# Eight heads scored and mixed in a row over one ring of seven PSUM banks, and a weight fetch placed anew, in a six-layer decoder

## The reference

```python
def attn_layer(x, Wqkv, qs, ksc, Wo):          # HEADS 16, DIM_HEAD 64, WINDOW 64
    q, k, v = split_heads(x @ Wqkv)
    q, k = l2norm(q) * qs, l2norm(k) * ksc
    q, k = rotary(q), rotary(k)                # tables of cos and sin, with a scale along the tokens
    out = local_attention(q, k, v)             # each token sees the 64 before it
    return out @ Wo

def ffn_layer(x, g, bln, W1, b1, W2, b2):      # DIM_INNER 682
    xn = layernorm(x) * g + bln
    a, gate = split(xn @ W1 + b1)
    return a * gelu(gate) @ W2 + b2

for i in range(6):
    x = attn_layer(shift_tokens(x), Wqkv[i], q_scale[i], k_scale[i], Wo[i]) + x
    x = ffn_layer(shift_tokens(x), ln_g[i], ln_b[i], W1[i], b1[i], W2[i], b2[i]) + x
return x
```

## Time and profile before

| | us |
|---|---|
| median of 3 runs | 2654.38 (2652.9 to 2655.96) |
| the profiled execution, its own time | 2655.91 |
| its span, first to last instruction | 2654.1 |
| TensorE busy | 2580.1 (97%), 25160 matmuls |
| VectorE busy | 2279.5 (86%) |
| ScalarE busy | 2059.5 (78%) |
| GpSimd busy | 1388.8 (52%) |
| mean granted TensorE clock | 0.994 of full speed |

### The profile page before, as it was taken

One profiled execution on the slowest core, in us unless ns is written; L12 is line 12 of the kernel. 1 busy time (PEld: TensorE's weight loads), 2 busy tenths in 40 slices (PEclk: granted clock), 3 DMA queues, 4 the chain that ended last, 5 costly groups with the idle time before them and its releaser, 6 DMA issues.

```text
span 2654.1 us, 77750 instructions
## 1 busy us (share of the span) xinstructions
PE 2580.1 (97%) x25160; PEld 2294.4 (86%) x25160; DVE 2279.5 (86%) x7689; ACT 2059.5 (78%) x6056; POOL 1388.8 (52%) x1438
## 2 busy tenths in 40 slices
PE   8889999999999999999999999999999999999996
PEld 7768888888888888888888888888888888888885
DVE  5579989988998888899888989988999998888883
ACT  5458878877887788788778878877887887787774
POOL 5454546455554645455454545545454555556560
PEclk9989999999999999999999999999999999999998
DMA  5212232424222333322234232243323242311100
GB/s 167 80 53 94 72 98 92 159 75 151 92 71 98 125 127 107 118 89 75 94 135 158 71 118 89 75 148 125 113 71 116 84 150 64 102 32 31 42 25 28
DMA packets 149542, 253.25 MB, mean 95 GB/s; under 512 B 21418, under 2 KB 88202, under 8 KB 148106
## 3 DMA queue, kind: packets, MB, share of 16 engines
q1 hardware_dynamic: 148698, 250.90, 29.1%
q10 hardware_dynamic: 688, 0.39, 0.0%
HBM read 137.14 MB, written 80.55 MB: 82 GB/s over the span
## 4 chain that ended last, share of the span: by engine, by line
PE 88%; DVE 3%; issue 2%; DMA 1%; POOL 1%; ACT 1%; SPq 1%; DVEq 0%; ACTq 0%; POOLq 0%
PE ring L1133 29%; PE ring L1183 14%; PE acc L1158 10%; PE score L1224 7%; PE ring L1237 6%; PE acc L1196 6%; PE ring L1147 6%; PE mix L1251 4%; PE mix L1255 2%; PE mix L1253 2%; PE ring L1167 1%; DMA xn<-res 1%; PE ring L1115 1%; PE acc L1203 0%; DVE probs L1609 0%
## 5 line engine op out<-in xcount | busy, mean ns | idle before, releaser
L1133 PE MATMUL ring<-w_qkv,xT 128*128 128x512 f32 x3456 | 883.0, 400 | 5.4 <-DVE with_sin L1516 4.0
L1133 PEld LDWEIGHTS ring<-w_qkv,xT 128*128 128x128 f32 x3456 | 624.0, 189 | 131.8 <-DVE with_sin L1516 5.4
L1418 POOL TENSOR_SCALAR sums_sq<-sums_sq 128x8 f32<-128x8 f32 x384 | 108.5, 283 | 1052.2 <-DVE sums_sq L1511 1043.9
L1354 ACT ACTIVATE probs<-probs,shift 128x128 f32<-128x128 f32 x1536 | 596.6, 392 | 26.5 <-DVE shift L1593 25.8
L1593 DVE CUSTOM_DVE_ANT_0 probs<-score,mask,query_scale 128x128 f32<-128x128 f32 x1536 | 438.7, 347 | 42.4 <-PE score L1224 35.0
L1183 PEld LDWEIGHTS ring<-nT,w_up 128*128 128x128 f32 x3168 | 395.8, 189 | 21.5 <-issue 6.8
L1183 PE MATMUL ring<-nT,w_up 128*128 128x256 f32 x3168 | 409.6, 282 | 4.3 <-issue 3.6
L1299 ACT ACTIVATE with_sin<-ring 128x512 f32<-128x512 f32 x384 | 228.2, 595 | 213.4 <-PE ring L1133 213.4
L1427 POOL TENSOR_TENSOR sums_sq<-sums_sq,half 128x8 f32<-128x8 f32 x192 | 324.4, 1690 | 16.0
L1424 POOL TENSOR_TENSOR query_scale<-sums_sq,half 128x8 f32<-128x8 f32 x192 | 318.0, 1656 | 22.0 <-POOL sums_sq L1418 11.8
L1372 ACT COPY probsT<-ring 128x512 f32<-128x512 f32 x384 | 226.1, 594 | 108.4 <-issue 103.0
(11 more groups left out here) (153 smaller groups left out, 4419.8 us busy)
## 6 DMA issues: line engine op xcount, KB each, us to landing
w_parts_scratch<-staging SPq DMA_DIRECT2D x120, 519.0 KB, 3.1
staging<-in_w_next SPq DMA_DIRECT2D x60, 519.0 KB, 4.9
w_qkv<-w_parts_scratch SPq DMA_DIRECT2D x20, 1536.0 KB, 9.4
v_mid<-v SPq DMA_DIRECT2D x192, 128.0 KB, 2.3
w_up<-w_parts_scratch SPq DMA_DIRECT2D x20, 640.0 KB, 6.9
y_in<-y_scratch SPq DMA_DIRECT2D x48, 256.0 KB, 3.0
res<-y_scratch SPq DMA_DIRECT2D x48, 256.0 KB, 2.8
y_scratch<-res SPq DMA_DIRECT2D x41, 256.0 KB, 3.2
```

Of the source, the lines that this page charges most:

```text
L1133: last = pe.matmul(bank(item)[:], xT[a][:, h, t * P:(t + 1) * P], w_qkv[w][:, h, c, g, :], start=(h == 0 and (a, w) == PASSES[0]), stop=(h ...
L1354: last = act.activation(probs[:, k, cols], probs[:, k, cols], ACT.Exp, bias=shift[:, k, i:i + 1], scale=-1.0, accum_out=sums[:, k, i:i + 1])
```

## The change

Three PSUM tensors go (two `score`, one `mix`) and their banks join the ring, which has seven now. The scores of a quad take two places in it, a mix takes one. `probs`, `probsT`, `shift` and `sums` hold eight heads instead of four. In `PE_ORDER` two quads are scored in a row, and behind them two are mixed in a row: at the start of a slot quads 0 and 1 are scored and quads 2 and 3 of the slot before are mixed; in the middle quads 2 and 3 are scored and quads 0 and 1 mixed. The lists of all engines are ordered anew around this. The first chunk of a slot's pair is loaded at the end of the slot before. The rotary tables are double, loaded at the start of the switch slot, and multiplied on GpSimd. The added tokens of the last layer (`x2`) are loaded ahead of `rest_parts`. `fetch(0)` moves behind the three shifted copies. The item `gelu_table` in `ACT_ORDER` has no instruction of its own.

```diff
-RING = 4
+RING = 7
 PE_ORDER = [
-    ("scores", 0), ("mix", 3), ("unit", 1, 0), ("unit", 1, 1), ("project_out", 0), ("unit", 1, 2), ("unit", 1, 3),
...
+    ("scores", 0),
+    ("scores", 1), ("mix", 2), ("mix", 3), ("unit", 1, 0), ("unit", 1, 1), ("unit", 1, 2), ("unit", 1, 3), ("project_out", 0),
+    ("project_out", 1), ("unit", 1, 4), ("unit", 1, 5), ("input",), ("turn", 1, 2), ("turn", 1, 0), ("turn", 1, 1),
+    ("turned", 0, 0), ("turned", 0, 1), ("turned", 1, 0), ("unit", 0, 0), ("turned", 1, 1), ("turn", 1, 3), ("norm_turn",),
+    ("scores", 2),
+    ("scores", 3), ("mix", 0), ("mix", 1), ("unit", 0, 1), ("gate", 0), ("gate", 1), ("unit", 0, 2), ("gate", 2), ("value", 0),
...
+RING_BANK = [_at % RING for _at in range(len(RING_FILLS))]
...
-    def load_chunk(self, sp, layer, chunk, h):
-        wait(sp, self.chunk_stored, self.chunk_at(layer, chunk, 0) * 32 + 1)
-        sp.dma_start(self.chunk_views(h)[0], self.D["w_next"][layer][:, chunk + h, :]).then_inc(self.raw_loaded, 16)
+    def load_chunk(self, sp, layer, chunk, h, first=False):
+        if not first:
+            wait(sp, self.chunk_stored, (self.chunk_at(layer, chunk, h) - 1) * 32 + 1)
+        sp.dma_start(self.chunk_views(h)[0], self.D["w_next"][layer][:, chunk + h, :]).then_inc(self.raw_loaded[h], 16)
...
+def build_tables(eng, layer, scales_loaded, tables_loaded, tables_built, tables, qk_scales):
+    eng.wait_ge(scales_loaded, layer * 16 + 16)
+    eng.wait_ge(tables_loaded, layer * 16 + 16)
+    for part in range(2):
+        scale = qk_scales[:, part].unsqueeze(1).broadcast_to([P, TILES, 2, HEAD_DIM // 2])
+        for k, sc in ((0, scale), (1, scale[:, :, ::-1, :])):
+            made = tables[layer % 2][:, 2 * part + k].rearrange("p t (a b) -> p t a b", a=2)
+            last = eng.tensor_tensor(made, made, sc, ALU.mult)
+    last.then_inc(tables_built, 1)
...
-        score = [ctx.enter_context(nc.psum_tensor(f"score{i}", [P, GROUP], FP32)) for i in range(2)]
-        mix = ctx.enter_context(nc.psum_tensor("mix", [P, 2, TOKENS], FP32))
...
+                if s.switch == "projections":
+                    load_tables(s.layer + 1)
+                    load_scales(s.layer + 1)
                 if s.early and not (isinstance(n, int) and n == -1):
...
-                    for h in range(SLOT_CHUNKS):
-                        W.load_chunk(sp, s.layer, s.chunk, h)
-                if s.switch == "projections":
-                    fetch(0, s.layer)
-                    load_scales(s.layer + 1)
+                    if isinstance(n, int) and n == 1:
+                        W.load_chunk(sp, s.layer, s.chunk, 0, first=True)
+                        W.load_chunk(sp, s.layer, s.chunk, 1, first=True)
+                    else:
+                        W.load_chunk(sp, s.layer, s.chunk, 1)
                 if s.ffn:
                     wait(sp, acc_read, f * 2 + 1 + 1)
...
                     sp.dma_start(xn[0:1, 1, P:DIM], res[P - 1:P, 0, P:DIM]).then_inc(shifted, 16)
+                if s.switch == "projections":
+                    fetch(0, s.layer)
...
+                if s.chunk is not None and s.more:
+                    W.load_chunk(sp, s.layer, s.chunk + SLOT_CHUNKS, 0)
...
+                elif kind == "scores":
+                    pe.wait_ge(scores_masked, n * HEADS + QUAD_HEADS * item[1] + QUAD_HEADS)
+                elif kind == "mix":
+                    k = item[1] if item[1] < 2 else item[1] - 4
+                    pe.wait_ge(out_split, n * PAIRS + 2 * k + 2)
...
-                wait(pe, scores_masked, H)
-                pe.sem_inc(passed, 1)
+                for half in range(2):
+                    bank_free(s, item, half)
+                    pe.sem_inc(passed, 1)
...
+                if s.switch == "projections":
+                    build_tables(pool, s.layer + 1, scales_loaded, tables_loaded, tables_built, tables, qk_scales)
                 for item in POOL_ORDER:
```

More of the change, by code:

```diff
@@ L79 @@
+    ("turned", 3, 1),
 ]
 ACT_ORDER = [
[L81 to L84 removed]
@@ L88 @@
+    ("copied", 2, 1), ("scale", 3, 0), ("value", 2), ("unit", 0, 5), ("turn", 0, 2), ("turn", 0, 1), ("turn", 0, 0),
     ("turn", 0, 3), ("copied", 3, 0), ("copied", 3, 1),
@@ L138, in is_filled @@
         return -1 <= n < STEPS - 1
-    if kind == "turned":
+    if kind in ("turned", "scores") or kind == "mix" and item[1] < 2:
         return 0 <= n < STEPS
@@ L217, in run_slots @@
             slot(Slot(layer * BATCH + 1, layer, next_batch=2, ffn_batch=0, chunk=0 if layer < DEPTH - 1 else None, new=True))
-        with eng.Fori(1 if layer and not apart else 2, BATCH - 1) as b:
+        with eng.Fori(1 if layer and not apart else 2, BATCH - 2 if apart else BATCH - 1) as b:
             slot(Slot(layer * BATCH + b, layer, next_batch=b + 1, ffn_batch=b - 1, chunk=(b - 1) * SLOT_CHUNKS if layer < DEPTH - 1 else None))
+        if apart:
+            b = BATCH - 2
+            slot(Slot(layer * BATCH + b, layer, next_batch=b + 1, ffn_batch=b - 1, chunk=(b - 1) * SLOT_CHUNKS if layer < DEPTH - 1 else None,
+                      more=False))
         if layer < DEPTH - 1:
@@ L850, in layers @@
         qk_scales = sb("qk_scales", [P, 2, 2, HEAD_DIM // 2])
-        tables = sb("tables", [P, 4, TILES, HEAD_DIM])
+        tables = [sb(f"tables{i}", [P, 4, TILES, HEAD_DIM]) for i in range(2)]
         y_in = T["y_in"]
@@ L1223, in quad_scores @@
                             at = k * BAND + (w // 2) * P
-                            last = pe.matmul(score[side][sides[w % 2], at:at + P], qT[rows, pair, w * WINDOW:(w + 1) * WINDOW],
+                            last = pe.matmul(bank(item, side)[sides[w % 2], at:at + P], qT[rows, pair, w * WINDOW:(w + 1) * WINDOW],
                                              kT[rows, pair, first:first + P], start=True, stop=True)
@@ L1378, in copy_out @@
                     wait(act, attn_projected, s.n)
[L1379 removed]
+                act.copy(oT[0][:, pair:pair + 2, :], wide_bank(("mix", item[1]))).then_inc(out_high, 2)
             def slot(s):
```

200 lines of the change are left out of this document (91 added, 109 removed).

## The result

The changed kernel takes **2719.64 us** (median of 4 runs, 2719.17 to 2720.84), the kernel before 2654.64 (4 runs, 2652.9 to 2655.96): ratio 1.0244, 95% interval 1.0231 to 1.0256. It is slower, as forecast, but by 65 us and not by 20; 2719.6 lies outside 2650 to 2700. The profiled execution took 2720.84, its span is 2718.9.

What follows compares the result with a forecast made beforehand. TensorE's list of work was taken to bound the slot (busy 51.22 of 51.57 us). Terms of -26 - 4 - 2 + 52 = +20 gave 2674 us, 0.7% slower, range 2650 to 2700.

Steps and rivals of the forecast that it cites:

- Part 4: Five layer-switching slots: TensorE waits 8.5 us for the later weight fetch, low clock costs 1.9; 10.4 a slot, +52 us.
- part 3: New waits on ScalarE: 0.34 before the second head pair, 0.86 before the quad 2 scores; +1.20 us a slot.
- part 5: Small terms: five switch slots' excess gone, -4 us; other excess, -2; bank for quad 3 scores has 0.6 us in hand.
- The -2: Earlier chunk load, earlier last-layer output addition and split semaphores remove part of the other 3.8 us excess: 0 to -4.
- Part 1: Every slot: fewer passages through scores and mixing, two joined passages saving 0.51 each; -1.02 us a slot.
- Part 2: Every slot: old waits at the mixing, the scaled heads and the normalized rows go; -0.75 us a slot.
- Net of parts 1 to 3: -0.57: Change per slot without the fetch: a slot of 51.0 us, -26 us over 46 slots.
- C: Rival: VectorE becomes the bound, slots stay at 51.6 or above, the fetch comes on top; up to 2705, chance 0.10.
- A: Rival: the fetch in the switch slots is not waited for; 2622 us, chance 0.13.
- B: Rival: ScalarE is not late and the fetch costs its lower bound; slots of 50.2, 2626 us, chance 0.07.
- D: Rival: both sides cancel, -0.9 a slot and 8 us fetch wait without clock loss; within 6 us of before, chance 0.08.

Runs made afterwards that it cites:

- Experiment 1: The run fetch_first: the changed kernel with only fetch(0) back at its old place, 2673.59 us.
- split_late_root: knot_root with VectorE's first split of the weights moved behind the rotation of unit (0, 1): 2644.29 us, ratio 0.9964 to the kernel before.
- fetch_first: The changed kernel with fetch(0) back ahead of the wait for the attention addition, nothing else: 2673.59 us, ratio 1.0066 to the kernel before.
- knot_three: Kernel of experiment 3 with the scale_ahead edit, two ScalarE copies made sooner, and VectorE's first weight split behind the normalization's application: 2660.72 us.
- split_late: knot_three with VectorE's first split of the weights moved behind the rotation of unit (0, 1): 2650.72 us, ratio 0.9991 to the kernel before.
- gpsimd_lighter: fetch_first with two of GpSimd's query-scale roots replaced by a cheap operation, so the reference is not computed: 2668.76 us.
- knot_root: knot_three with one query-scale root on GpSimd moved behind the root of the normalization: 2650.99 us, ratio 0.9983 to the kernel before.
- experiment 3: fetch_first with the scores' wait for the copied turns placed behind the two waits for free banks: 2657.22 us, ratio 1.001 to the kernel before.
- scale_ahead: Kernel of experiment 3 with ScalarE scaling head pair (0, 1) behind unit (1, 3) and no longer behind the input: 2653.36 us.
- experiments 7 to 10: The four runs knot_three, knot_root, split_late and split_late_root, reordering VectorE's and GpSimd's lists: 2660.72, 2650.99, 2650.72 and 2644.29 us.

## Why the prediction was wrong, point by point

**Direction and the largest term: right.** Part 4 gave 10.4 us a switch slot and +52. Measured: slots of 62.46, 62.69, 62.24, 62.30 and 62.31, 10.1 to 10.5 above the 52.17 of ordinary ones, +49.9 against the same intervals before. By its pieces, 8.5 of idle time and 1.9 of clock were forecast, and 9.10, 9.6, 9.1, 8.8, 8.8 of idle time came out. In the first of them TensorE is busy 52.70, 2.03 more than in the ordinary slot; the unit, the transposes and the turn behind it account for it (2.73 + 0.84 + 0.86 between starts, against 1.48 + 0.44 + 0.44). So the low clock costs about 2.0, and 0.8 of that is not seen in the length, since the waits of part 3 shrink beside it (10.3 = 9.1 + 2.0 - 0.8). The landing took 11.6 against the 10.9 taken, inside the bounds of the earlier trace rows. Experiment 1 gives the term as 46, with the wait gone. The -4 of part 5 was put down to the shift copies being free of the fetch's traffic, and no run shows that: in split_late_root the five slots take 51.92, 51.41, 51.38, 51.39 and 51.52, no more than its others, with the fetch ahead of the copies. What took the excess away are edits of GpSimd's roots: fetch_first, knot_three and split_late, which differ from gpsimd_lighter, knot_root and split_late_root in these alone, spend 4.8, 3.9 and 4.8 us more in the five slots. In them GpSimd builds the tables, four operations of 0.48 us, in front of its rotations. Part 5 had named that danger and put no price on it; that the building is what makes these slots longer is argued, not shown. The -2 is not resolved either; the 4.8 saved at the end of the kernel was not forecast.

**Part 1: the mechanism stands, its size in part.** The scores of two quads take 1.91 from start to start (1269.51 to 1271.42), the two mixings 1.95 (1271.42 to 1273.37); 1.90 and 1.95 were forecast. One quad of scores and its mixing took 2.09 between starts before (1450.15 to 1452.24), so a joined passage saves 0.32. The other 0.20 of the 0.51, the slower start of the unit behind, was read from 1.59 against 1.38 in the earlier trace rows, which are pieces of a chain: between starts that unit took 1.49 before (1452.24 to 1453.73) and takes 1.50 now (1273.37 to 1274.87). No run shows this term as a saving. An estimated 0.16 us for three changes of tiling, from the pages of the Trainium skill weighed there (TensorEngine Tiling (Array Packing), Key Properties, and TensorE: Matmul & The Clock Gate, Part 2), is half of the 0.32 that a joined passage saves.

**Part 2: right where it was looked at.** The waits of the earlier trace rows before the mixing are gone. But only 0.35 of the 1.77 of parts 1 and 2 was idle time, so TensorE's busy time should have fallen by 1.42, and it fell by 0.55. Of the 0.87 between, 0.70 are the slow starts behind the new waits, which count as busy.

**Part 3: the step that failed.** "Net of parts 1 to 3: -0.57" became +0.48, worth 43 us over the 41 slots and almost the whole error. The new waits were put at 1.20 a slot. By the distances between starts in the ordinary slot shown, less the 0.44 of a group of transposes, they cost 2.20: 0.45 at the scaled pair (0.34 forecast), 0.75 at the normalized rows (nothing), 0.57 at the scores of quad 2 (0.86) and 0.43 at the scores of quad 0 (nothing).

That a late normalization "hides behind this wait" was right, and the wait it hides behind was sized too small. In the 23 slots in which GpSimd's root takes 1.41, the rows lose 0.75 and the scores of quad 2 0.57; in most of the others the rows lose 0.15 and the scores 1.18. The sum is 1.32 in both kinds of slot, since the copy of the last turn sets the start of the scores. The forecast for this sum was 0.86 (its own terms, 0.2 + 4 x 0.48 + 0.1 less 1.31, give 0.91). With the wait placed last, in experiment 3, it is 1.04 in the median slot. So 0.28 of the miss is what the queue does between release and first matmul. The rest is mostly a slower start of the scores behind the rows, which lasts 0.14 even where nothing is waited for.

The scores of quad 0 were counted as met, and by the copy they were: in the slot shown it ended at 1243.43, and TensorE came at 1243.54. They lost 0.38 in the median slot all the same, and 0.09 in experiment 3, so the order of the waits is the cause here too. Experiment 3 measured both places together: 16.4 us of time.

Of the 1.17 us by which the slot missed 51.0, the waits are 1.00, the slower start that part 1 saved on paper 0.40, and two groups of 24 gate matmuls 0.14 (2.88 each, 2.81 before; the cause is open). The other pieces are shorter by 0.37 in sum.

**The rivals.** C (slots at 51.6 or above, up to 2705) was nearest in size, and its mechanism is wrong as it was put: VectorE works 46.90 of 52.17, no more than before, and with the same work slots of 51.45 were reached. What C had right is where VectorE stands: not its sum, but its order behind the normalization, which experiments 7 to 10 found. A is excluded by the waits for `w_qkv`, B (slots of 50.2) and D by the ordinary slots.

**My theory of the knot.** It said that the scores start at the latest of three chains. scale_ahead bears it out (4 us, not 18). It was one chain short: VectorE's rotation of unit (0, 0), on which the prediction's part 5 counted 0.6 us in hand. Once the other three end sooner, the 0.6 is gone, and knot_three spent it on a split. Where TensorE still idles 0.76 a slot is named above, and not removed: to start the root of the normalization sooner was not tried beyond knot_root.

## What to carry to other kernels

A fetch that is issued behind a wait must be dated by its landing, and its user by the new order: both moved here, and 46 us is what the meeting costs. Waits in a row that end at one event have one sum: to shorten the first lengthens the next (1.32 us here in both kinds of slot). Write down for each point the time at which every chain arrives, ahead of deciding what an edit is worth, and include the chain that has "something in hand". Of several waits ahead of one instruction, put the one that comes last in time last in order.

## What was not expected of the hardware

**Restart after a wait.** With two waits on banks and their increments still ahead of the scores, TensorE began the scores of quad 2 0.29 to 0.48 us after the end of the copy, 0.38 or 0.39 in most slots; with that wait last, 0.10 in all 41 that waited. The load of the first 64x64 tiles is not what differs: from it to the first matmul it is 0.03 in both (1269.48 to 1269.51, 1291.12 to 1291.16), and it begins 0.35 behind the copy in the one and 0.06 in the other. Which of the two waits and the two increments takes how much of the 0.28, no run separates.

**GpSimd's root of two elements** takes 713 ns at the least, 800 in the median and 1409 at the most in the changed kernel:

```profile
L1470 POOL TENSOR_TENSOR ln_rstd<-ln_mv,half x48: 713/800/1409, 201.8 to 2692.3; 128x2 f32<-128x2 f32 x48
```

In the slot shown above it took 1.41, and VectorE subtracted two SBUF tiles for 0.69 of that (L352, from 1266.03). The difference to the least is 0.70. In 23 of the 48 slots the root takes 1.41, each time with this subtraction begun 0.15 behind its start; seven more have the subtraction beside them and take 0.80; no root without it takes more than 0.80. In the runs in which the split stands elsewhere, none takes more than 0.84. Here is split_late:

```profile
L1469 POOL TENSOR_TENSOR ln_rstd<-ln_mv,half x48: 715/797/802, 200.4 to 2617.9; 128x2 f32<-128x2 f32 x48
```

So the subtraction is what lengthens the root. The Trainium skill (SBUF — State Buffer, SBUF: two separate sides) says that VectorE with two SBUF inputs and GpSimd contend for a pair of ports, that the one that starts first holds it for the whole instruction, and that the other blocks. The rows agree in size and not in who waits: the root's record begins first (1265.88), and it is the root that grew by 0.70, while VectorE's operation took 0.68 to 0.70 in all 120 cases. When within its record GpSimd takes the ports, no run shows. In the changed kernel this cost nothing, since the copy of the turn bound anyway (the sum of 1.32 above).

**Two transfers 2.8 us apart share the way.** The fetch of group 1, issued 2.8 us behind that of group 0, kept SyncE for 4.17 us where group 0's two issues took 1.10, and the two 128 KB copies issued between them, `v_mid`, took 10.6 and 11.0 us to land, against a median of 2.3 in the whole kernel. The landing of all `w_qkv` transfers has a median of 12.8 us, before 9.4.
